# Delta stage of a one-core layer kernel: row factors ahead of the scans, key projections in two banks, corner products one stage later, no unit-matrix products in the first level

## What is computed

```python
mixed = hidden_states @ w_qkv
z = (hidden_states @ w_z).reshape(B, S, HV, DV)
b, a = hidden_states @ w_b, hidden_states @ w_a
y = conv_general_dilated(x, conv_w, padding=[(KCONV - 1, 0)], feature_group_count=CONV_DIM)
mixed = jax.nn.silu(y).transpose(0, 2, 1)
beta = jax.nn.sigmoid(b)
g = -jnp.exp(A_log) * jax.nn.softplus(a + dt_bias)
q = _l2norm(q) * DK ** (-0.5)
k = _l2norm(k)
def step(Sm, inp):
    q_, k_, v_, g_, b_ = inp
    Sm = Sm * jnp.exp(g_)[..., None, None]
    kv = jnp.einsum('bhk,bhkv->bhv', k_, Sm)
    delta = (v_ - kv) * b_[..., None]
    Sm = Sm + jnp.einsum('bhk,bhv->bhkv', k_, delta)
    return (Sm, jnp.einsum('bhk,bhkv->bhv', q_, Sm))
_, o = jax.lax.scan(step, S0, (qt, kt, vt, gt, bt))
og = o * jax.nn.silu(z)
on = og * jax.lax.rsqrt(mean(og * og) + EPS) * norm_w
return on.reshape(B, S, VAL_DIM) @ w_out
```

## Time and profile before

| | |
|---|---|
| median of 3 runs | 5850.61 us |
| the profiled execution: its time | 5859.23 us |
| its span | 5857.5 us |
| delta loop (64 stages) | 230 to 3195 us of the span |
| one cycle | 180.9 to 192.5 us |
| its four stages in a clean cycle | 48.5, 47.1, 46.4 and 38.9 us |
| mean granted TensorE clock | 0.918 |

### The profile page before, as it was taken

One profiled execution on the slowest core, in us unless ns is written; L12 is line 12 of the kernel. 1 busy time (PEld: TensorE's weight loads), 2 busy tenths in 40 slices (PEclk: granted clock), 3 DMA queues, 4 the chain that ended last, 5 costly groups with the idle time before them and its releaser, 6 DMA issues. The chain is left out here.

```text
span 5857.5 us, 141443 instructions
## 1 busy us (share of the span) xinstructions
PE 5015.8 (86%) x58860; PEld 3526.0 (60%) x58910; DVE 3106.0 (53%) x5375; ACT 2753.3 (47%) x7449; POOL 1612.4 (28%) x1859
## 2 busy tenths in 40 slices
PE   5699998999889998899987899799978696499969
PEld 4477676776667676776766555455555354255545
DVE  4465656565565565655565566455552554443231
ACT  2355555556555555555554444344441344324521
POOL 0244443444444344443443000111100321012210
PEclk7799999999999999999999899899989698688879
DMA  2000000000000000000001000100000000000000
GB/s 86 20 20 18 20 19 21 20 18 15 23 22 20 15 19 20 24 20 15 19 20 33 26 1 1 67 1 0 0 21 14 15 1 14 22 1 1 1 22 15
DMA packets 51142, 106.61 MB, mean 18 GB/s; under 512 B 12960, under 2 KB 20032, under 8 KB 49376
## 3 DMA queue, kind: packets, MB, share of 16 engines
q1 hardware_dynamic: 50528, 97.84, 5.5%
HBM read 90.20 MB, written 5.52 MB: 16 GB/s over the span
## 5 line engine op out<-in xcount | busy, mean ns | idle before, releaser
L1223 POOL TENSOR_TENSOR dh_qi<-dh_lv,dh_ids 128x256 f32<-128x256 f32 x640 | 553.3, 869 | 1293.1 <-ACT dh_lv L929 1293.1
L929 ACT ACTIVATE dh_lv<-bank 128x384 f32<-128x384 f32 (+1 forms) x1280 | 531.2, 468 | 371.2 <-PE bank L719 258.5
L1045 DVE SCALAR_TENSOR_TENSOR dh_kq<-bank,dh_conv_kq,dh_kq 128x511 f32<-128x511 f32 (+2 forms) x408 | 305.5, 749 | 264.3 <-ACT dh_kq L885 254.7
L719 PEld LDWEIGHTS bank<-dh_lv 64*64 64x64 f32 x14336 | 257.3, 134 | 203.7 <-issue 183.0
L627 PE MATMUL bank<-hT,dh_w_kq 128*128 128x512 f32 x544 | 278.4, 636 | 86.5 <-DVE dh_kq L1045 78.8
L719 PE MATMUL bank<-dh_lv 64*64 64x64 f32 x14336 | 326.8, 225 | 17.7 <-ACT dh_lv L929 17.2
L1045 DVE SCALAR_TENSOR_TENSOR dh_v<-bank,dh_conv_v,dh_v 128x511 f32<-128x511 f32 (+2 forms) x384 | 285.5, 747 | 94.5 <-ACT dh_v L885 85.4
L810 PE MATMUL bank<-dh_wo_gated,dh_ww 128*128 128x256 f32 x1040 | 289.4, 426 | 49.3 <-DVE dh_qkm L1088 49.3
L301 POOL TENSOR_TENSOR ln_rstd<-ln_var_eps,nhalf 128x16 f32<-128x16 f32 x8 | 23.2, 2903 | 1050.1 <-DVE ln_var_eps L291 1050.1
L719 PE MATMUL bank<-dh_lv,dh_qi 64*64 64x64 f32 x10240 | 278.7, 225 | 16.9 <-POOL dh_qi L1223 16.8
L1759 PE MATMUL bank<-moe_h_split,moe_w 128*128 128x512 bf16 x1150 | 265.8, 380 | 17.2 <-PEq L89 14.6
(11 more groups left out here) (422 smaller groups left out, 11965.9 us busy)
## 6 DMA issues: line engine op xcount, KB each, us to landing
dh_rates<-delta_rates SPq DMA_DIRECT2D x130, 256.0 KB, 3.5
dh_w_vz<-in_L_wvz SPq DMA_DIRECT2D x17, 512.0 KB, 3.5
mod_w<-in_L_wmod SPq DMA_DIRECT2D x4, 1536.0 KB, 7.7
dh_w_kq<-in_L_wkq SPq DMA_DIRECT2D x18, 256.0 KB, 2.6
dh_wo<-in_L_wo SPq DMA_DIRECT2D x16, 256.0 KB, 4.1
moe_w<-in_L_w13T SPq DMA_DIRECT2D x1, 3200.0 KB, 16.0
later_gates<-mod_gate SPq DMA_DIRECT2D x3, 1024.0 KB, 4.0
gate<-later_gates SPq DMA_DIRECT2D x6, 512.0 KB, 3.5
```

Of the source, the lines that this page charges most:

```text
L719: last = pe.matmul(lvl[g][halves[g ^ o], sl, kind, :], lhs, w[:, kind, :], start=True, stop=True)
L929: last = act.activation(lv[:, j, r, :, kinds, :], lvl[r][:, :, kinds, :], ACT.Copy)
L1045: dve.scalar_tensor_tensor(y, pj_bank(n)[:, 0:S - i], taps(n)[:, TAPS - 1 - i:TAPS - i], y, ALU.mult, ALU.add).then_inc(s["v_cs" if i < TA ...
L1223: pool.tensor_tensor(qi[j][:, :, :, :].rearrange("p r s n -> p (r s) n"), lv[:, j, :, :, :, :].rearrange("p r s k n -> p (r s) k n")[:, :, ...
```

## The change

Five edits, all in the delta part but the last:

1. **DVE's order** at a stage's end: `normed` directly behind `kk_mask`, `qk_mask` behind the side item and the vectors, then `decay`, `start_power`, `collect`.
2. **Banks of the keys**: of the four key items, the second and the fourth use the bank TURN, so that `project` waits for the item two back. `cross` of that stage waits for the last key convolution. Ahead of the loop keys and queries alternate between PJ_A and PJ_B.
3. **Corner products**: `corner` and `corner_copy` of stage t go behind `turn_c` and `c_copy` of head 0 in stage t + 1 (the last stage of a pass keeps them). The stage's first side item goes in front of the second head's turn.
4. **First level**: the product with the unit matrix that added one to the partial inverse is dropped. GpSimd's `plus` of level 1 adds the unit matrix to both the transposed power and the partial inverse (128x512 instead of 128x256), and level 1 reads the inverse from there.
5. Masks that only the setup needs, and the matrix of ones, are no longer kept for the whole kernel; each part that needs ones sets its own.

```diff
-    qi = [sb(f"qi{j}", [P, 2, 2, HALF]) for j in HEADS]
+    qi = [sb(f"qi{j}", [P, 2, 2, 2, HALF]) for j in HEADS]
...
-    def pj_bank(n):
-
-        return bank[PJ_B if n < V_ITEMS and n % 2 else PJ_A][:, :]
+    def pj_bank(q, n):
+
+        if n % 2 and (n < V_ITEMS or q < 0):
+            return bank[PJ_B][:, :]
+        return bank[TURN if n in (V_ITEMS + 1, V_ITEMS + 3) else PJ_A][:, :]
...
-        elif n <= V_ITEMS:
+        elif q < 0 or n <= V_ITEMS + 3:
             after(pe, s["v_cv"], N - 1)
+        elif n == V_ITEMS + 4:
+            pe.wait_ge(s["v_cv"], N - 1)
         else:
             pe.wait_ge(s["v_cv"], N)
+        if q >= 0 and n in (V_ITEMS + 1, V_ITEMS + 3):
+            pe.wait_ge(hs[1]["a_ct"], NC * q + 2)
...
         for kind in (POW, TPOW, INV):
             for sl in range(2):
-                for more in range(2 if kind == INV else 1):
-                    for g in range(2):
-                        for o in range(2):
...
-                            one = ids[halves[g], :]
-                            lhs, rhs = ((cT, c), (c, cT), (one if more else cT, one))[kind]
...
+                        lhs, rhs = ((cT, c), (c, cT), (cT, ids[halves[g], :]))[kind]
...
-                        lhs = (w[:, TPOW, :], w[:, POW, :], qi[j][halves[g], g ^ o, sl, :])[kind]
...
+                        plus_one = qi[j][halves[g], g ^ o, sl, :, :]
+                        lhs = (w[:, TPOW, :], w[:, POW, :], plus_one[:, 0, :])[kind]
+                        rhs = plus_one[:, 1, :] if i == 1 and kind == INV else w[:, kind, :]
...
         for j in HEADS: pe.wait_ge(hs[j]["a_x"], t + 1)
+        if t % NC == 1: pe.wait_ge(s["v_cv"], count(t // NC, V_ITEMS + 4))
...
         turn_c(pe, t, 0)
+        if t: corner(pe, t - 1)
         v_turn(pe, t, 0)
         if old:
             for j in HEADS: ks(pe, t, j)
+        side_tensor(pe, q, a, 0)
         turn_c(pe, t, 1)
         v_turn(pe, t, 1)
-        side_tensor(pe, q, a, 0)
...
         c_copy(act, t, 0)
+        if t: corner_copy(act, t - 1)
         v_scaled(act, t, 0)
+        side_scalar(act, q, a, 0)
         c_copy(act, t, 1)
         v_scaled(act, t, 1)
-        side_scalar(act, q, a, 0)
...
         kk_mask(dve, t)
-        for j in HEADS: decay(dve, t, j)
+        for j in HEADS: normed(dve, t, j)
         side_vector(dve, q, a, 7)
         if a == 2: key_vectors(dve, q)
         if a == 3: query_vectors(dve, q)
-        for j in HEADS: normed(dve, t, j)
+        qk_mask(dve, t)
+        for j in HEADS: decay(dve, t, j)
         for j in HEADS: start_power(dve, t, j)
-        qk_mask(dve, t)
         collect(dve, t)
...
+        out = qi[j][:, :, :, :, :].rearrange("p r s k n -> p (r s) k n")
+        src = lv[:, j, :, :, TPOW:INV + 1, :].rearrange("p r s k n -> p (r s) k n")
+        if i == 1:
+            one = mask_bc(ids[:, :], 2 * NB).rearrange("p (b k) n -> p b k n", k=2)
+            pool.tensor_tensor(out, src, one, ALU.add).then_inc(h["p_qi"], 1)
+        else:
+            pool.tensor_tensor(out[:, :, 0, :], src[:, :, 0, :], mask_bc(ids[:, :], NB), ALU.add).then_inc(h["p_qi"], 1)
```

More of the change, by code:

```diff
@@ L115, in __init__ @@
         self.blockneg_h = sb("mask_block_half", [P, P], BF16)
-        self.ones = sb("ones", [P, P])
         self.nhalf = sb("nhalf", [P, 2 * NB * NC])
@@ L139, in _ @@
             def _(dve):
-                dve.memset(k.ones[:, :], 1.0).then_inc(consts, 1)
                 dve.memset(k.nhalf[:, :], -0.5).then_inc(consts, 1)
@@ L143, in _ @@
                 dve.wait_ge(loaded, 16 * 8)
-                for half, full in ((k.ident_h, k.ident), (k.causal_h, k.causal), (k.blockneg_h, k.blockneg)):
+                for half, full in ((k.ident_h, k.ident), (k.causal_h, causal), (k.blockneg_h, blockneg)):
                     dve.tensor_copy(half[:, :], full[:, :]).then_inc(consts, 1)
@@ L156, in modulations @@
         cbc = ph.sb("cbc", [P, LAYERS, KD, NB, P])
+        ones = ph.sb("ones", [P, P])
+        ones_s = ph.sem("ones")
         raw = ph.sb("raw", [P, 4, 2 * D])
@@ L189, in _ @@
                 act.wait_ge(silu, 1)
+                act.wait_ge(ones_s, 1)
                 def broadcast(l):
@@ L193, in broadcast @@
                         for b in range(NB):
-                            last = act.activation(cbc[:, l, kk, b, :], k.ones[:, :], ACT.Copy,
+                            last = act.activation(cbc[:, l, kk, b, :], ones[:, :], ACT.Copy,
                                                   scale=cT[:, l, kk, b:b + 1])
@@ L234, in _ @@
             def _(dve):
+                dve.memset(ones[:, :], 1.0).then_inc(ones_s, 1)
                 for l in range(LAYERS):
@@ L372, in delta_gates @@
         exT = ph.sb("exT", [P, 4, P])
+        ones, ones_s = ph.sb("ones", [P, P]), ph.sem("ones")
         loaded, proj, taken, rate_s = ph.sem("loaded"), ph.sem("proj"), ph.sem("taken"), ph.sem("rate")
@@ L401, in _ @@
                 g = gates[:, :, 0, :, :].rearrange("p h c b -> p h (c b)")
-                for i, m in enumerate((k.le, k.gt, k.ones)):
+                pe.wait_ge(ones_s, 1)
+                for i, m in enumerate((k.le, k.gt, ones)):
                     pe.matmul(k.bank[4 + i][:, :].rearrange("p (h c) -> p h c", h=H), m[:, :], g, start=True,
@@ L626, in project @@
         for kk in range(KD):
-            last = pe.matmul(pj_bank(n), w[:, kk, :], k.hT[:, kk, n % NB, :], start=(kk == 0), stop=(kk == KD - 1))
+            last = pe.matmul(pj_bank(q, n), w[:, kk, :], k.hT[:, kk, n % NB, :], start=(kk == 0), stop=(kk == KD - 1))
         last.then_inc(s["t_pj"], 1)
@@ L646, in turn_kq @@
             after(pe, s["a_z"], 2 * NC * q + 4)
+            after(pe, s["v_cv"], K_ITEMS + Q_ITEMS if q < 0 else 0)
             pe.wait_ge(s["a_si"], count(q, V_ITEMS + K_ITEMS))
@@ L686, in first_level @@
             for sl in range(2):
-                for more in range(2 if kind == INV else 1):
-                    for g in range(2):
-                        for o in range(2):
-                            c = ci[j][halves[g], 2 * sl + o, halves[g]]
-                            cT = ct[j][halves[g], 2 * sl + o, halves[g]]
-                            one = ids[halves[g], :]
-                            lhs, rhs = ((cT, c), (c, cT), (one if more else cT, one))[kind]
-                            last = pe.matmul(lvl[g][halves[g ^ o], sl, kind, :], lhs, rhs, start=(more == 0),
-                                             stop=(kind != INV or more == 1), skip_group_check=True)
+                for g in range(2):
+                    for o in range(2):
+                        c = ci[j][halves[g], 2 * sl + o, halves[g]]
+                        cT = ct[j][halves[g], 2 * sl + o, halves[g]]
+                        lhs, rhs = ((cT, c), (c, cT), (cT, ids[halves[g], :]))[kind]
+                        last = pe.matmul(lvl[g][halves[g ^ o], sl, kind, :], lhs, rhs, start=True, stop=True)
         last.then_inc(h["t_lv"], 1)
@@ L723, in level @@
                     last = pe.matmul(lvl[o][halves[o], sl, POW, :], lv[halves[o], j, 0, sl, INV, :],
-                                     qi[j][halves[o], 0, sl, :], start=True, stop=True)
+                                     qi[j][halves[o], 0, sl, 0, :], start=True, stop=True)
         last.then_inc(h["t_lv"], 1)
@@ L871, in tensor_stage @@
         cross(pe, t)
-        corner(pe, t)
+        if t == STAGES - 1: corner(pe, t)
     def tap(act, q, n):
```

16 lines of the change are left out of this document (6 added, 10 removed).

## The result

The changed kernel takes **5578.6 us** (median of 4 runs, 5573.4 to 5583.2), the kernel before beside it 5855.9 us (4 runs). The ratio is 0.9521, with a 95% interval of 0.949 to 0.9553: 277 us faster. The forecast was 5605 us, in a range of 5545 to 5700. The profiled execution took 5583.2 us, with a mean granted clock of 0.927.

A forecast was written before the change was run, and what follows sets the result against it. The delta loop was taken to run at TensorE's pace, with time to gain from its waits, dropped products and clock. Terms summed to 242 us off a 5850.6 us median, 5608, stated as 5605 us, range 5545 to 5700.

The forecast's parts named there:

- ahead of the loop: Eight key and query items before the delta loop: with two banks 3.7 us each instead of 6.9, 21 us gained.
- Normed rows and masks: TensorE's waits at stage ends: 60.9 and 49.3 us go, a new first-stage query-mask wait costs 15 us.
- The clock: TensorE's granted clock in the loop rises as waits go: 19 us behind the normed-rows wait, 22 us elsewhere.
- Fourth stage's wait for GpSimd: Fourth stage: half of the 1.05 us wait for a GpSimd addition that overlapped the scans goes, 8 us.
- Keys' banks: Second stages: key projections wait for the convolution two back, so all 56.9 us of waits go.
- Unit products: First level: 2048 dropped matmuls save 30 us of TensorE's time on the path; GpSimd's longer addition costs 3 us.
- Corner: Corner products one stage later take the same time, and the turn inherits their 0.48 us wait: nothing gained.
- Side item: Stage starts: second stages gain 13.2 and 6 us; the other three get a `z_prod` wait, 26 us in all.
- Everything goes: Rival, chance 0.12: no new `z_prod` or mask wait and the clock's full 36 us, giving 5553 us.
- GpSimd holds VectorE: Rival, chance 0.12: GpSimd's injections slow scans and start powers in each stage, 102 us back, 5710 us.
- Two banks bring nothing: Rival, chance 0.08: key waits only move to the tap or next level, 57 us stay, 5665 us.
- The start powers decide: Rival, chance 0.04: start powers, last on VectorE, delay each next stage's first turn, 320 us back, 5928 us.

## Why the prediction was right

The sign, the size and the places were right: 242 us forecast, 277 measured. The stages came at 43.6, 40.9, 44.3 and 37.7 us, against 44.5, 41.5, 44.2 and 38.1. The terms in the order of the sum; "measured" is what undoing the part cost, but for the row "ahead of the loop", which is read from the two traces and which no run undid.

| part | forecast, us | measured, us |
|---|---|---|
| VectorE's order with the clock and the fourth stage's wait | 60.9 - 15 + 49.3 + 19 + 22 + 8 = 144 | 180 (186 by itself) |
| keys in two banks, in the loop | 57 | 68 |
| ahead of the loop | 21 | 22 |
| unit products, less the longer addition | 30 - 3 = 27 | 15 |
| corner one stage later | 0 | -15 |
| side item ahead of the second turn | 13.2 + 6 - 26 = -7 | 0 |
| sum | 242 | 270 |

The parts measured leave 7 us of the 277 over, no more than executions vary by. The fifth edit, the masks and the ones, was put at nothing, and no run undid it; what it brings cannot be told apart from these 7 us.

- **Normed rows and masks.** Both waits went as forecast. The new one for the mask came where it was said, in first stages alone, at the lower bound of 0.3 to 1.4 us: 0.33 us, 5.2 in all, not 15. The normed rows took 1.28 us instead of 2.36, since the injections that stood beside them now come later, and the mask ended at 1085.7.
- **The clock** is the term that was most mis-sized: 19 + 22 = 41 us. Measured are 126 us less at 1.2 GHz, 63 us of work at most. Summing the time at half speed over the loop of the kernel before gives 146.8 us, 73 us lost: the bound could have been read there. By the clock records 81.9 of them start at the 16 waits of 3.1 us, 30.7 at waits of 2.3 us, 13.7 at the fourth stage's two waits of 1.1 us and 20.5 at the ends of three passes. "Two thirds of the way to the slower" was about right: the faster cycle has 3.4 us at 1.2 GHz, the slower 13.7, the loop's mean is 9.2. Three steps made the term too small. The 10.2 us by which the two cycles differ were priced at 3.4 us, the difference of their lengths, and not at half, 5.1. Of the 36 us that gave, 14 were taken off for the ends of passes, where only 20.5 us at 1.2 GHz stay, 10 us of work. And "part of it fell into idle time" took 1.65 us to 1.2, while the trace has that stretch behind the wait, with TensorE busy 3.21 of the 3.5 us (length, busy times and clock as in the earlier trace rows):

```profile
1193.00:1197.40 4.40, 0.77 (x12) 0.42 (x4) 4.33 (x6) 1.12 (x3) 3.84 (x4) 1.00 0.39 119
1197.40:1200.90 3.50, 3.21 (x31) 2.59 (x32) 2.04 (x4) 1.71 (x8) 0.00 (x0) 0.51 0.00 0
```

- **Fourth stage's wait for GpSimd**. I took half, since normed rows come where the scans were. All 15.7 us went. The longer addition brought a wait of its own of 2.6 us, forecast at 3.
- **Keys' banks.** Mechanism right, all 48 waits gone. The term was read off the wait, and a wait shown as 1.18 us is worth 1.45 from start to start.
- **Ahead of the loop.** Items came each 6.9 us and come each 3.59 us now (3.7 forecast):

```profile
153.68 2.32 DVE L1058 SCALAR_TENSOR_TENSOR dh_kq<-bank,dh_conv_kq,dh_kq 128x511 f32<-128x511 f32 x3 [1.27 <-ACT dh_kq L897]
156.05 1.98 PE L637 MATMUL bank<-hT,dh_w_kq 128*128 128x512 f32 x4 [1.61 <-DVE dh_kq L1058]
157.27 2.31 DVE L1058 SCALAR_TENSOR_TENSOR dh_kq<-bank,dh_conv_kq,dh_kq 128x511 f32<-128x511 f32 x3 [1.27 <-ACT dh_kq L897]
```

  The projection itself takes 1.98 instead of 3.78 us, at full clock now. In one bank it stood in the chain of each item, so up to 1.8 of the 3.3 us that an item gained may be the clock's and not the second bank's; no run parts the two.
- **Unit products.** The duration was right, "on the path" was not: half of them stood where TensorE waits anyway, since my own next step put a wait behind them. Two terms of the sum met in one place and were added. (The 2048 of the prediction are records, two to a matmul; the 30 us hold.)
- **Corner.** "Nothing there" failed: the wait moved to the turn and grew by 0.1 us, and the turns around the corner products take 0.06 us more each, 0.2 us four times a cycle.
- **Side item.** The new wait at the second `z_prod` was forecast at 26 us and is 20.8, 0.45 us in first, third and fourth stages:

```profile
1055.62 0.69 DVE L1126 TENSOR_TENSOR dh_x<-dh_x,dh_vs 128x512 f32<-128x512 f32 x1 [2.91 <-ACT dh_vs L928]
1056.37 1.16 PE L609 MATMUL bank<-dh_x,dh_ttb 128*128 128x128 f32 x8 [0.47 <-DVE dh_x L1126]
```

  By stage lengths it costs 1.54 us a cycle, 25 us, and the gain at the second stage's front is 17 us, against 19. Net that is a loss of 7.5 us, against 7; the totals, equal within what executions vary by, cannot show it.

**The rivals.** "Everything goes" (5553 us) was right about the clock, near on the mask and wrong about `z_prod`. "GpSimd holds VectorE" (5710 us) was right about the start powers and wrong about the time: their pair grew from 1.28 to 2.91 us, and the run with later injections shows that this is hidden. Its other pair, the scans, stayed at 2.33 us in the first stage shown; over the loop their mean rose from 1.21 to 1.39 us, which later injections did not change. The Trainium skill, "SBUF — State Buffer", section "Who interferes with whom", has a VectorE instruction with two SBUF inputs and a GpSimd instruction that reads SBUF exclude each other for a whole instruction; the trace agrees: 1.28 us of start powers took 2.91 us beside injections, which took 3.32 instead of 2.04 us themselves. "Two banks bring nothing" (5665 us) fell: one bank costs 68 us. "The start powers decide" (5928 us) needed them 6.5 us late; made 2.84 us late they cost 98 us, so the gain would have been undone by some 2.84 + 180 / 64 = 5.7 us, an estimate that takes each further microsecond in full. Nothing made them so late.
